# Four orders changed in a fused attention and expert kernel: base product behind the second low-rank product, relu ahead of exponentials, lower q/k part ahead of the last division, expert output by token pairs

## The reference

```python
h = layernorm(x) * (1 + ca) + sa
q, k, v = split(h @ W_attn + b_attn)            # 16 heads of 16 channels
phi(z) = exp(z @ omega - 0.5 * |z|^2) / sqrt(128)   # 128 features, on q/4 and k/4
y = (phi(q) . cumsum(phi(k) v)) / (phi(q) . cumsum(phi(k)) + eps)
x = x + ga * (y @ W_proj + b_proj)

h = layernorm(x) * (1 + cb) + sb
w = softmax(h @ Wg.T + bg), only the two largest of four kept
base = h @ Wi.T                                  # 1024 hidden
hid[e] = relu(base + (h @ A[e].T) @ B[e].T)      # rank 4, experts e = 0..3
x = x + gb * sum_e w[e] * (hid[e] @ Wo.T)
```

## Time and profile before

| | |
|---|---|
| median of 3 runs | 792.42 us (791.97 to 794.87) |
| the profiled execution | 791.14 us, of which the span from its first to its last instruction is 788.9 us |
| granted TensorE clock over the span | 0.991 |
| block period, loop | about 91.25 us |
| TensorE busy | 740.5 us, 94% |
| VectorE busy | 526.3 us, 67% |
| ScalarE busy | 422.1 us, 53% |
| DMA queue | 30.6% of 16 engines' span |

### The profile page before, as it was taken

How to read it: one execution, slowest core, us unless ns; L and a number is a source line. 1 busy time by engine, 2 the same in 40 slices (tenths; PEclk the granted TensorE clock), 3 DMA queues, 4 the chain that set the end, 5 groups by cost and what they waited for, 6 DMA issues and landing times.

```text
span 788.9 us, 17005 instructions
## 1 busy us (share of the span) xinstructions
PE 740.5 (94%) x6138; PEld 605.5 (77%) x6138; DVE 526.3 (67%) x1265; ACT 422.1 (53%) x769; POOL 62.7 (8%) x72
## 2 busy tenths in 40 slices
PE   3889999999999999999999999999999999999696
PEld 3678768887698867887688876987678876987466
DVE  4366776676666776766776767767766767766456
ACT  3376636664556554665366745575456644564232
POOL 1260010001000010001000010000100010000100
PEclk9999999999999999999999999999999999999799
DMA  8750183103801065102811057010741029000000
GB/s 282 198 143 2 54 211 64 53 0 118 205 2 53 27 188 111 53 0 80 208 38 53 0 146 179 9 44 27 212 87 53 0 89 223 13 29 28 0 1 27
DMA packets 42804, 65.36 MB, mean 83 GB/s; under 512 B 5000, under 2 KB 19104, under 8 KB 42656
## 3 DMA queue, kind: packets, MB, share of 16 engines
q1 hardware_dynamic: 42784, 65.09, 30.6%
HBM read 39.91 MB, written 25.17 MB: 82 GB/s over the span
## 4 chain that ended last, share of the span: by engine, by line
PE 79%; DVE 12%; issue 3%; DMA 2%; ACT 2%; POOL 1%; DVEq 0%; SPq 0%; ACTq 0%; POOLq 0%
PE pa L579 11%; PE prod L592 7%; PE ring L428 6%; PE ring L558 5%; PE pa L428 5%; PE pa L430 5%; PE pa L429 5%; PE ring L430 4%; PE ring L429 4%; PE ring L612 4%; PE ring L563 3%; PE ring L720 2%; PE ring L619 2%; PE pa L693 2%; DVE am_phk L1178 2%
## 5 line engine op out<-in xcount | busy, mean ns | idle before, releaser
L579 PE MATMUL pa<-phq,phkT 128*128 128x128 f32 x768 | 101.2, 275 | 0.0
L1178 DVE TENSOR_TENSOR am_phk<-pa,const 128x512 f32<-128x512 f32 x112 | 77.0, 688 | 35.6 <-PE pa L579 34.6
L579 PEld LDWEIGHTS pa<-phq,phkT 128*128 128x128 f32 x768 | 95.4, 192 | 2.1
L1348 DVE SCALAR_TENSOR_TENSOR am_phk<-ring,am_phk 128x512 f32<-128x512 f32 x64 | 44.3, 691 | 53.2 <-PE ring L773 53.2
L988 ACT ACTIVATE qk_r<-phq 128x512 fp32r<-128x512 f32 x64 | 40.5, 633 | 63.7 <-DVE phq L1357 63.7
L428 PE MATMUL pa<-wo_r,qk_r 128*128 128x256 f32 x256 | 72.2, 282 | 0.6 <-DVE qk_l L1353 0.6
L430 PE MATMUL pa<-wo_l,qk_r 128*128 128x256 f32 x256 | 72.3, 282 | 0.0
L429 PE MATMUL pa<-wo_r,qk_l 128*128 128x256 f32 x256 | 72.0, 281 | 0.0
L558 PE MATMUL ring<-xq,omega_x 100*128 100x512 f32 x196 | 70.3, 440 | 1.4 <-DVE lora_w L1171 1.4
L918 ACT ACTIVATE phq<-ring 128x512 f32<-128x512 f32 x82 | 49.3, 602 | 36.1 <-PE ring L558 34.9
L918 ACT ACTIVATE phkT<-ring 128x512 f32<-128x512 f32 x98 | 58.3, 595 | 12.9 <-PE ring L558 12.6
(11 more groups left out here) (209 smaller groups left out, 1609.3 us busy)
## 6 DMA issues: line engine op xcount, KB each, us to landing
xq<-qk_parts SPq DMA_DIRECT2D x48, 512.0 KB
qk_parts<-qk_r SPq DMA_DIRECT2D x32, 256.0 KB, 4.4
qk_parts<-qk_l SPq DMA_DIRECT2D x32, 256.0 KB, 4.9
tok<-in_L_attn_x SPq DMA_DIRECT2D x8, 512.0 KB, 3.6
xr<-in_L_attn_x SPq DMA_DIRECT2D x8, 512.0 KB, 3.4
out_x<-tg SPq DMA_DIRECT2D x16, 256.0 KB, 2.2
norm_parts<-norm_r SPq DMA_DIRECT2D x16, 128.0 KB, 2.3
norm_parts<-norm_l SPq DMA_DIRECT2D x16, 128.0 KB, 2.4
```

The costliest lines, as they stand in the source:

```text
L579: mm = pe.matmul(score_bank(q, a)[:, tt], phkT[:, q % 2, a, tt], query(q)[:, a, tt], start=True, stop=True)
L1178: dve.tensor_tensor(am[:, 2 * (q % 2) + a, :].rearrange("p (c t) -> p c t", c=NT), score_bank(q, a)[:].rearrange("p (c t) -> p c t", c=NT) ...
L1348: dve.scalar_tensor_tensor(r2[:, f % 2, :], z_bank[f % 4][:], 0.0, rho, ALU.max, ALU.mult).then_inc(r2_done.sem, 1)
```

## The change

It has five edits. The first two belong together.

- TensorE, expert stage: base(f + 2) moves behind z2(f - 1) and the feature tiles of the iteration. `AHEAD` becomes {0: 1, 1: 1, 3: 2, 4: 1, 5: 1, ...}: the two tiles of iteration 2 come in iteration 3 and that of iteration 3 in iteration 4.
- ScalarE, expert stage: in iteration f it takes the exponentials of the tiles of iteration f - 1, so that they stand behind relu(f); what is left is taken after the loop.
- TensorE: the masks are made between the two halves of base(3), not behind it.
- VectorE: `split_qk(n + 1, 1)` stands ahead of the division of the last group.
- VectorE: `finish` goes by token pairs. It waits for the first pair's output products (a new semaphore, set behind the last product of `pa[0]`), scales two groups, adds the residual, and then does the same for the second pair.

```diff
-AHEAD = {0: 1, 1: 1, 2: 2, 3: 1, 5: 1, 6: 1, 7: 1, 8: 1, 9: 2, 10: 1}
+AHEAD = {0: 1, 1: 1, 3: 2, 4: 1, 5: 1, 6: 1, 7: 1, 8: 1, 9: 2, 10: 1}
@@ TensorE, ffn_head
                 wait(pe, low_high, n, 1)
-                base(n, 3)
+                base(n, 3, [0])
+                masks(n)
+                base(n, 3, [1])
@@ TensorE, experts
                         ratio(n)
-                    if 4 <= f + 2 < FT:
-                        base(n, f + 2)
                     if 1 <= f <= FT:
...
                             features(n + 1, tile // TILES, [tile % TILES])
                             tile += 1
+                    if 4 <= f + 2 < FT:
+                        base(n, f + 2)
                     if f >= 3:
...
+                            if k == FT - 1 and t == 1:
+                                mm.then_inc(wo_first.sem, 1)
                         mm.then_inc(wo_mm.sem, 1)
@@ TensorE, after_attend
                 ffn_head(n, front_next)
-                masks(n)
                 experts(n, front_next)
@@ ScalarE, ffn
-                    for _ in range(AHEAD.get(f, 0) if front_next else 0):
+                    for _ in range(AHEAD.get(f - 1, 0) if front_next else 0):
                         features(n + 1, tile // TILES, [tile % TILES])
                         tile += 1
...
+                while front_next and tile < 2 * TILES:
+                    features(n + 1, tile // TILES, [tile % TILES])
+                    tile += 1
@@ VectorE, attend
                 add_reads(n, GROUPS - 1)
+                if front_next:
+                    split_qk(n + 1, 1)
                 divide(n, GROUPS - 1)
-                if front_next:
-                    split_qk(n + 1, 1)
@@ VectorE, finish
-                wait(dve, wo_mm, n, FT)
-                for t in range(NT):
-                    dve.scalar_tensor_tensor(tg[:, t // 2, t % 2 * C:(t % 2 + 1) * C],
-                                             pa[t // 2][:, t % 2 * C:(t % 2 + 1) * C], w1[:, t:t + 1], gb_now,
-                                             ALU.mult, ALU.mult).then_inc(scaled.sem, 1)
                 for b in range(2):
+                    if b == 0:
+                        wait(dve, wo_first, n, 1)
+                    else:
+                        wait(dve, wo_mm, n, FT)
+                    for t in (2 * b, 2 * b + 1):
+                        dve.scalar_tensor_tensor(tg[:, t // 2, t % 2 * C:(t % 2 + 1) * C],
+                                                 pa[t // 2][:, t % 2 * C:(t % 2 + 1) * C], w1[:, t:t + 1], gb_now,
+                                                 ALU.mult, ALU.mult).then_inc(scaled.sem, 1)
                     wait(dve, scaled, n + 1, 2 * b + 2)
```

More of the change, by code:

```diff
@@ L272, in build @@
         r2_done, g_sum, g_high, g_low = (sig(name, FT) for name in ("r2_done", "g_sum", "g_high", "g_low"))
-        wo_mm, fin = sig("wo_mm", FT), sig("fin", 2)
+        wo_mm, wo_first, fin = sig("wo_mm", FT), sig("wo_first", 1), sig("fin", 2)
         scaled = sig("scaled", NT)
@@ L1259, in attend @@
                 add_reads(n, GROUPS - 1)
-                divide(n, GROUPS - 1)
                 if front_next:
                     split_qk(n + 1, 1)
+                divide(n, GROUPS - 1)
             def residual(n):
```

## The result

The changed kernel takes **804.3 us** (median of 6 executions, 801.96 to 806.43) against 792.5 for the kernel before beside it: a ratio of 1.0143, interval 1.0116 to 1.0169. It is slower. The forecast was 805.4, range 797.5 to 810. The medians differ by 11.8 us, where the forecast has 13.0. The profiled execution's span is 802.1 us, 13.2 more than before; that is not the size of the change, since the two profiled executions had different mean granted clocks (0.991 before, 0.986 now), as the last sections show.

The account below looks back on a forecast made before the run. TensorE, busy 94%, was taken as the bound. Seven blocks at -0.69 + 2.85 = +2.16 give +15.1, the last block -2.1, together +13.0: 804.1 us profiled, 805.4 as median, range 797.5 to 810.

Parts of the forecast that it names:

- Masks: Between base(3)'s halves, the masks fill TensorE's stand ahead of the expert stage: -0.69 us per block.
- Tile 0: First feature tile waits for the DMA of the norm rows: 0.2 us taken, between 0 and 0.69.
- The walk of the stage: Expert stage timed step by step from its first low-rank product: 27.90 us instead of 25.05, +2.85 per block.
- z2(1): Second low-rank product of hidden tile 1, TensorE: waits 0.16 us, for relu(1) on ScalarE.
- z2(2): Second low-rank product of hidden tile 2, TensorE: waits 0.32 us, for relu(2) on ScalarE.
- Tile 4's stand: TensorE at feature tile 4 waits for tile 2's exponential, now behind relu(4): 1.11 us, plus 0.1 restart.
- tile 10's: TensorE at feature tile 10 waits for tile 8's exponential, now behind ScalarE's last rounding: 1.5 us, plus 0.1 restart.
- the exponentials are no bound: Faster rival, expert stage: exponentials are over when TensorE arrives, only the shortened chain stays; 781 us, chance 0.07.
- The q/k part: VectorE's step ahead of the last division fits its gap, projection ends the same: 0, bounds -0.2 and +0.2 us.
- Output by token pairs: VectorE's expert output: a loop block gains 0, only the kernel's end gains 0.5 us.
- The last block: No features, so no new wait: masks -0.6, stage ends 1.0 sooner, store 0.5; together -2.1 us.
- The clock rival: Each block's new stands halve the granted clock, +1.8 us or so each: 818 us, chance 0.03.

Follow-up runs that it names:

- masks_only: Kernel before with only the masks moved between the two halves of base(3): 789.0 us against 793.3 for the kernel before.
- act_back: Changed kernel with ScalarE's exponentials back in their own iteration, behind its relu: 783.7 us against 793.3 for the kernel before.
- act_only: Kernel before with ScalarE's edit alone, exponentials of iteration f - 1 behind relu(f): 812.7 us against 794.2 for the kernel before.
- tile10_late: Changed kernel with feature tile 10 moved from iteration 9 to iteration 10: 794.1 us against 793.3 for the kernel before.
- qk_only: Kernel before with only the lower q/k part ahead of the last division: 790.5 us against 794.2 for the kernel before.
- finish_only: Kernel before with only the expert output by token pairs: 792.3 us against 794.2 for the kernel before.

## Why the prediction was right, and where not

**Masks: right.** -0.69 at z1(0) in masks_only, to the hundredth. **Tile 0: right as a mechanism, too small in size.** 0.2 was taken; masks_only shows 0.19 and the changed kernel 0.09 to 0.54, on average 0.38. The difference comes with the q/k part's gain, which arrives at the same wait.

**The walk of the stage: right.** z2(1) was to wait 0.16, and z1(2) to z2(1) is 0.39, so 0.16. z2(2) was to wait 0.32 and waits 0.29 (402.26 to 402.78 in the changed kernel's timeline, less 0.23). Tile 4's stand was put at 1.11 and is 1.10, tile 10's at 1.5 and is 1.50. The stage was to take 27.90 and takes 27.7 to 28.1. (In the stage of the kernel before the prediction's terms add up to 23.9, not 23.8; nothing in the forecast's sum hangs on it.) That the stands belong to ScalarE's order is shown by act_back from one side and act_only from the other; that they add is shown by tile10_late. The rival "the exponentials are no bound" (781) needed just act_back's one edit more: it measures 783.7.

**The q/k part: wrong.** Forecast 0 with bounds of -0.2 and +0.2; qk_only shows -0.31. The failed step was that the projection stands for ScalarE's second copy after two of its 0.21 us products. Each of the eight products is two records, 0.22 us apart: sixteen in all in qk_only's row above, while the row ends after twelve, at its window's edge. So the part that needs only the first copy is four records long, 0.86 us, and lasts until the second copy is there: TensorE goes on with it at 371.97 in qk_only, 0.09 later than without any wait. In the changed kernel the step had little effect, as most of the gain went on into tile 0's wait.

**Output by token pairs: right.** 0 in the loop, 0.6 at the end where 0.5 was forecast.

**The last block: right, although the two profiles hide it.** Its stage went from 24.52 to 23.49 us (z1(0) to the start of the last product), 1.0 shorter as walked, at a granted clock of 1.00 in both. But the whole block up to its last product took 91.27 us against 91.64, when 1.6 less was forecast for that part. The difference lies ahead of the stage, in the granted clock. In windows of 10 us of the kernel before:

```profile
730.00:740.00 10.00, 7.42 (x62) 6.09 (x61) 3.91 (x11) 1.19 (x2) 2.35 (x1) 0.83 0.00 0
740.00:750.00 10.00, 5.56 (x16) 3.13 (x14) 5.49 (x18) 3.02 (x5) 1.38 (x2) 0.70 0.00 0
750.00:760.00 10.00, 9.49 (x44) 6.65 (x44) 5.59 (x27) 2.31 (x6) 0.00 (x0) 0.96 0.01 2
```

and of the changed kernel:

```profile
740.00:750.00 10.00, 6.43 (x86) 4.42 (x79) 4.54 (x13) 0.60 (x1) 0.00 (x0) 0.81 0.17 54
750.00:760.00 10.00, 6.11 (x26) 4.72 (x24) 5.07 (x19) 1.39 (x3) 3.73 (x3) 0.84 0.00 0
760.00:770.00 10.00, 9.29 (x30) 5.56 (x29) 4.30 (x15) 3.91 (x7) 0.00 (x0) 0.66 0.01 2
```

The third figure from the end is the mean granted clock. The granted clock is at full or at half in these records, so a window at share c of the full clock had 2 x (1 - c) x 10 us at half. That is 3.4 + 6.0 + 0.8 = 10.2 us before, and 3.8 + 3.2 + 6.8 = 13.8 after, 3.6 us more. It is not the change that brings them. finish_only, act_only and qk_only work this stretch exactly as the kernel before does, and they took 92.85, 93.13 and 93.03 us for it, at a granted clock of 0.93 like the changed kernel. These are the rows of finish_only and of the changed kernel, from the block's first scores to its last product:

```profile
691.98:784.83 92.85, 82.24 (x677) 66.15 (x676) 54.82 (x132) 36.32 (x67) 4.70 (x4) 0.93 0.04 12
705.53:796.80 91.27, 82.07 (x677) 66.03 (x676) 54.84 (x132) 36.65 (x67) 4.70 (x4) 0.93 0.04 13
```

So at an equal clock the block is 1.6 to 1.9 us shorter, where 1.6 was forecast, and it is the profile of the kernel before that had drawn less slow clock than all others but tile10_late's.

**The clock rival: not seen where it was feared.** In the loop the stands of 1.1 and 1.5 us left the granted clock at 1.00 (the stage's window above). But the prediction's account of the kernel before is short of one stretch. Ahead of the slow one that it names, behind the stand of 3.7 us, the window of 730 to 740 above has 3.4 us at half clock too, and there no stand was longer than 1.6 us; TensorE had several in a row:

```profile
729.64 0.66 PE L603 MATMUL ring<-const,prod_sb 128*128 128x128 f32 x4 [1.05 <-DVE tg L1209]
731.90 1.08 PE L612 MATMUL ring<-phq,s_sb 128*32 128x128 f32 x32 [1.60 <-DVE state L1194]
733.79 1.11 PE L619 MATMUL ring<-const,s_sb 128*128 128x128 f32 x4 [0.81 <-DVE s_sb L1198]
```

So the length of the loop's stands alone was no safe argument; that there is dense work between them was the better one. The Trainium skill ("TensorE: Matmul & The Clock Gate", Part 1) has the throttled clock as the default that activity lifts; the trace agrees in that these slow stretches lie in the last block, where TensorE works with gaps, and that the dense loop has none (1.00 from 143.8 to 691.3 us of the kernel before).

**The sum.** Seven periods were to grow by 15.1 and grew by 13.9 (640.4 to 654.3 us from the first to the last block's start). From the second block on z1(0) came 1.00 us sooner and not 0.69, for the q/k part, and the stage took 2.94 more on average and not 2.85, mainly for tile 0's wait. The last block and the end were to give back 2.1; at an equal clock they gave back 1.6 to 1.9 and, behind the last product, 0.6. That makes 11.4 to 11.7, and the medians differ by 11.8, where 13.0 was forecast. So the forecast's median is 1.1 too high, and it is the loop's 1.2. This error would have been larger if the q/k part's 0.31 had not partly gone into tile 0's longer wait; that much is luck.

The spans of the two profiled executions differ by 13.2, and that this is so near 13.0 is luck as well. The changed kernel's profile had 3.6 us more slow clock in the last block, worth some 1.2 us by the comparison with finish_only (92.85 against 91.64), and a start of the first block 0.3 later (51.24 against 50.92; the ten profiles have 50.4 to 51.4 there). The mean clock of the whole execution says the same: 791.14 us at 0.991 before, at the fast end of what this kernel does (790.87 at 0.991 to 795.53 at 0.983 in nineteen other executions), and 804.32 at 0.986 now.

## What to carry to other kernels

Where a bank is used in turn, find for every product that reuses it the last step that reads the bank, and what stands ahead of that step in its own engine's order. A cheap step put behind one that waits for the very engine it serves turns a free hand-over into a full round trip, here 1.2 and 1.6 us in each block, although no engine got more work. A gain ahead of a wait for a transfer is worth only what the transfer leaves: two gains of 0.57 and 0.31 together were worth 0.54. And before two profiled spans are compared, their granted clocks are to be compared.

## What was not expected of the hardware

The last block, where TensorE has no next-block work to fill in, draws a different share of slow clock in each profile, though its program is the same. tile10_late and the changed kernel have the same instructions there, yet from that block's first scores to its last product they took 89.1 and 91.3 us. tile10_late's mean clock over it is 0.96, the changed kernel's 0.93 (its row is above):

```profile
695.35:784.45 89.10, 79.45 (x677) 64.06 (x676) 54.82 (x132) 36.65 (x67) 4.70 (x4) 0.96 0.04 13
```

That is 2 us between programs that don't differ there, a quarter of a per cent. It fits the spread of executions: the changed kernel's fastest, 801.96 us, had a mean clock of 0.990, its slowest, 806.43, one of 0.983. What decides how the slow stretches fall wasn't tried. The loop's periods don't have it, which is why they tell steps of 0.3 us apart that the medians can't, and why a difference of two profiled spans is not to be taken for the size of a change.
